# Cross-attention in a fused two-layer kernel: the sixth projection of a unit directly behind the fifth, both groups of outer key products behind it

## The reference

```python
q_hk  = (hidden_q @ Wq.T).reshape(Bv, Sv, H, K)          # H = 16 heads, K = 128
q_big = jnp.einsum('bshk,hkq->bshq', q_hk, w_kc_q)        # q = 192
q_big = _apply_rope(q_big, sin_q, cos_q)                  # rotary embedding
kv_r  = _apply_rope(kv_c, sin_k, cos_k)
q_r = jnp.einsum('bshq,hqr->bhsr', q_big, W_qr)           # r = 64
k_r = jnp.einsum('bld,hdr->bhlr', kv_r, W_kr)
attn = softmax(jnp.einsum('bhsr,bhlr->bhsl', q_r, k_r))
ctx_c = jnp.einsum('bhsl,bld->bhsd', attn, kv_r)
# then w_kc_kv, the heads side by side, and @ Wo.T
```

## Time and profile before

| | |
|---|---|
| median of 3 runs | 454.44 us (454.17 to 456.39) |
| profiled execution | 456.93 us, of which 455.1 us are the span |
| PE busy | 371.9 us, 82% of the span |
| DVE busy | 337.4 us, 74% |
| ACT busy | 212.2 us, 47% |
| POOL busy | 138.8 us, 31% |
| loop over the 8 units | about 212 to 363 us of the span |
| mean granted PE clock | 0.929 |

### The profile page before, as it was taken

How to read it: one execution, slowest core, us unless ns; L and a number is a source line. 1 busy time by engine, 2 the same in 40 slices (tenths; PEclk the granted TensorE clock), 3 DMA queues, 4 the chain that set the end, 5 groups by cost and what they waited for, 6 DMA issues and landing times.

```text
span 455.1 us, 10577 instructions
## 1 busy us (share of the span) xinstructions
PE 371.9 (82%) x3676; PEld 255.3 (56%) x3677; DVE 337.4 (74%) x858; ACT 212.2 (47%) x466; POOL 138.8 (31%) x149
## 2 busy tenths in 40 slices
PE   2578667832777788998999999999999989729995
PEld 1356555731344445776466475575664778616784
DVE  6968899888788989589677886886876525682453
ACT  1788999551577788684021231132132221324441
POOL 1100000023477774311092340440431410143334
PEclk9988999955599999998999999999999989957999
DMA  8995760402146551271022032032021101333011
GB/s 284 414 378 202 269 266 5 164 24 63 36 146 211 200 162 48 61 263 39 0 94 94 2 94 94 1 94 75 20 94 34 61 1 48 140 85 101 25 36 37
DMA packets 17183, 50.77 MB, mean 112 GB/s; under 512 B 2104, under 2 KB 6464, under 8 KB 15088
## 3 DMA queue, kind: packets, MB, share of 16 engines
q1 hardware_dynamic: 14272, 42.46, 25.9%
q0 software_dynamic: 2864, 7.68, 5.7%
HBM read 43.44 MB, written 6.69 MB: 110 GB/s over the span
## 4 chain that ended last, share of the span: by engine, by line
PE 58%; DVE 18%; ACT 9%; issue 7%; POOL 5%; DMA 2%; DVEq 0%; SPq 0%; ACTq 0%; POOLq 0%
PE bank L960 16%; PE bank L1174 8%; PE bank L976 6%; PE bank L1048 5%; PE bank L987 3%; ACT W L1207 2%; ACT pnat L1193 2%; PE bank L666 2%; PE bank L819 2%; PE bank L1001 2%; POOL y_rows L592 2%; PE bank L1027 2%; PE bank L1011 2%; PE bank L699 2%; PE bank L830 1%
## 5 line engine op out<-in xcount | busy, mean ns | idle before, releaser
L1722 DVE TENSOR_TENSOR roped<-bank,cst 128x512 f32<-128x512 f32 x96 | 61.1, 685 | 28.9 <-PE bank L960 27.9
L613 POOL TENSOR_TENSOR WE<-WE,wT 128x512 f32<-128x512 f32 x32 | 42.1, 1342 | 82.2 <-DMA WE<-_L_ffn_expert_masks_dram 82.2
L960 PE MATMUL bank<-XNT_hi,AW_hi 128*128 128x512 f32 x96 | 42.1, 438 | 0.0
L960 PE MATMUL bank<-XNT_lo,AW_hi 128*128 128x512 f32 x96 | 37.8, 394 | 0.0
L960 PE MATMUL bank<-XNT_hi,AW_lo 128*128 128x512 f32 x96 | 37.6, 392 | 0.0
L1341 ACT ACTIVATE qrT<-bank 128x512 f32<-128x512 f32 x16 | 8.7, 595 | 61.8 <-PE bank L987 61.8
L1048 PE MATMUL bank<-VW,ctxT 128*128 128x256 f32 x128 | 32.2, 399 | 0.0
L976 PE MATMUL bank<-roped,MW 128*64 128x512 f32 x128 | 31.0, 605 | 0.0
L1335 ACT ACTIVATE prob<-prob 128x512 f32<-128x512 f32 x16 | 10.1, 632 | 44.3 <-DVE prob L1732 44.3
L585 POOL DMA_INDIRECT xg<-x_rows,owner_b x23 | 22.7, 985 | 23.0 <-DVE owner_b L429 13.9
L960 PEld LDWEIGHTS bank<-XNT_hi,AW_hi 128*128 128x128 f32 x96 | 18.1, 188 | 19.4 <-issue 11.4
(11 more groups left out here) (306 smaller groups left out, 876.9 us busy)
## 6 DMA issues: line engine op xcount, KB each, us to landing
raw<-in_L_ffn_w_dram SPq DMA_DIRECT2D x8, 1536.0 KB, 8.4
fold<-in_L_xattn_fold_dram SPq DMA_DIRECT2D x8, 1024.0 KB, 5.6
WE<-_L_ffn_expert_masks_dram SPq DMA_DIRECT2D x8, 1024.0 KB, 5.4
kv<-in_keys_values_dram SPq DMA_DIRECT2D x8, 656.0 KB, 7.8
yg<-y_rows SPq DMA_DIRECT2D x8, 256.0 KB, 4.8
x_tok<-pay SPq DMA_DIRECT2D x8, 256.0 KB, 2.2
X<-in_x_dram SPq DMA_DIRECT2D x4, 256.0 KB, 9.9
x_rows<-xrow SPq DMA_DIRECT2D x1, 516.0 KB, 4.4
```

Source lines behind the costliest of these rows:

```text
L613: pool.tensor_tensor(WE[:, e], WE[:, e], wT[:], ALU.mult).then_inc(WE_ready, 1)
L960: mm = pe.matmul(bank[g][:], a[:, k, c * P:(c + 1) * P], b[:, k, g * 512:(g + 1) * 512], start=k == 0 and i == 0, stop=k == 1 and i == 2)
L1722: ins = dve.tensor_tensor(roped[n][:, r, :].rearrange("p (b s) -> p b s", s=S), src, cst[:, None, at:at + S].to_broadcast([P, 8, S]), ALU. ...
```

## The change

In PE's loop over the units, `project(u, 5)` is moved in front of `to_keys_outer(u, 0)`. Nothing else is changed, and no other engine's list.

```diff
@@ -1082,8 +1082,8 @@
                 project(u, 2)
                 project(u, 3)
                 project(u, 4)
+                project(u, 5)
                 to_keys_outer(u, 0)
-                project(u, 5)
                 to_keys_outer(u, 1)
                 to_keys_middle(u)
                 if u + 1 < NU:
```

## The result

The changed kernel takes 459.6 us (median of 4 runs, 457.96 to 462.76) against 454.31 us (4 runs, 454.13 to 456.39) on the same chip: a ratio of 1.0117, 95% interval 1.0076 to 1.0157, 5.3 us slower. The forecast was 460.1.

The account below looks back on a forecast made before the run. PE alone was taken to set the time in units 1 to 6, with DVE's work hidden. Units 1 to 6 +5.67, unit 0 -0.15, unit 7 +0.11: +5.63 on 454.44 gives 460.1 us, range 458.2 to 462.9.

Parts of the forecast that it names:

- The place and the kind of the wait: Units 1 to 7: projection 5, now directly behind projection 4, waits for rope 3 on DVE to free bank 1.
- The size of the wait: Unit 3: projection 5 starts 0.06 behind rope 3's end, at 272.91 instead of 271.96; the unit becomes 0.95 us longer.
- the sign to look for: Units 1 to 7: projection 5's load shows about 1.0 us of idle in front, released by rope 3.
- That it comes back in every unit: Units 1 to 6: rope 3 keeps its distance to the unit's start, so the wait recurs: 6 x 0.945 = 5.67 us.
- The joint of the two outer groups: Units 1 to 7: outer groups 0 and 1 back to back, up to 0.10 cheaper or dearer than 1.86; taken as 0.
- Unit 0: No wait, since no less_max stands ahead of rope 3; shorter by 0.10 to 0.20 from fewer matmul switches, taken as -0.15.
- Unit 7: Last unit of the loop: turn_probs starts at 350.85 instead of 350.74, +0.11 in place of 0.94.
- The turn from "DVE is late" to "PE is late": Unit 7: turn_probs stood idle 0.75 for by_sum; after the change probabilities are ready at 349.8 and PE is late.
- The sum: Whole kernel: 5.67 - 0.15 + 0.11 = +5.63 us, forecasting 460.1 us, 1.2% slower.
- The clock rival: Pauses of 0.95 in seven units lower PE's clock, up to 1.65 us each: 471.6 us; chance 0.05.
- the expert stage's 1.26 of idle without a drop: Evidence against the clock rival: from 145 to 147 PE idles 1.26 us and the clock stays at 1.00.
- The gain rival: No wait if rope 3 ends by 271.80 in unit 3: 8 x 0.15 + 0.75 = 1.95 us faster, 452.5; chance 0.05.

Follow-up runs that it names:

- two ways: Changed kernel with rope 3 moved before the second less_max on DVE: 0.9906; changed kernel with projection 5 and rope 5 in bank 7: 0.9883.
- both controls: Kernel before with rope 3 moved before the second less_max on DVE: 1.0030; kernel before with projection 5 and rope 5 in bank 7: 1.0000.
- rope 3 first: Changed kernel with the next unit's rope 3 moved on DVE in front of the second less_max: 452.23 us, ratio 0.9906.
- a free bank: Changed kernel with projection 5 and rope 5 in PSUM bank 7 instead of bank 1: 451.39 us, ratio 0.9883.
- the changed kernel with the 1.17 us operation: Changed kernel plus an unused 512-column multiplication by 1 on DVE before rope 3 of units 1 to 7: 469.60 us, ratio 1.0279.
- the one with 1.05: Changed kernel plus an unused 256-column multiplication by 1 on DVE before rope 3 of units 1 to 7: 469.96 us, ratio 1.0291.
- The three changed kernels with an added operation: Changed kernel plus an unused DVE operation before rope 3: 512-column multiplication by 1, 1.0279; 256-column, 1.0291; product of two SBUF operands, 1.0321.
- the kernel before with the 1.05 us operation: Kernel before plus an unused 256-column multiplication by 1 on DVE before rope 3 of units 1 to 7: 456.33 us, ratio 1.0034.
- The 512 columns: Unused 512-column multiplication by 1 on DVE before rope 3 of units 1 to 7: kernel before with it 1.0011, changed kernel with it 1.0279.
- the product: Unused product of two SBUF operands on DVE before rope 3 of units 1 to 7: kernel before with it 1.0052, changed kernel with it 1.0321.

## Why the prediction was right, point by point

**The place and the kind of the wait: right.** Projection 5 of units 1 to 7 waits for bank 1, released by rope 3. Shown by taking the wait away in two ways, and by both controls.

**The size of the wait: right.** I had rope 3's end + 0.06; it was 0.05. Projection 5 starts 5.56 behind projection 2 (275.76 - 270.20), where I had 272.91 - 267.33 = 5.58. Only the sign to look for was misstated: "about 1.0 us of idle" in front of projection 5's load is 1.29, and 0.86 in front of its matmul.

**That it comes back in every unit: right.** Rope 3 keeps its distance to projection 2, 4.23 before (271.56 - 267.33) and 4.22 after (274.42 - 270.20). The idle time that DVE has won went in front of the next unit's rope 0: 2.66 us in unit 3 (284.52), where the kernel before has 0.93 (280.84); 0.92 of it comes from rope 5, which waits 0.56 instead of 1.48.

**The joint of the two outer groups: mis-sized.** I took 1.86 + 1.87 = 3.73 and allowed 0.10 to either side; they take 3.58 together. With it the middle products start 10.73 behind projection 2 instead of 10.89. A unit costs 0.82 instead of 0.945, and the sum for units 1 to 6 is 4.9 instead of 5.67. The rows allow an estimate of the joint: eight outer matmuls more take 3.58 - 1.86 = 1.72, 0.215 each, so the step out of a group takes 1.86 - 7 x 0.215 = 0.36. Two groups in a row have one such step less, 0.36 - 0.215 = 0.14. The 1.86 that I took for a block held this step; the joint wasn't looked at by itself.

**Unit 0: -0.32 where I took -0.15.** The same 0.15 of the joint is what is missing.

**Unit 7: -0.03 where I took +0.11,** again short by the joint. The turn from "DVE is late" to "PE is late" came as worked out: the probabilities are ready 0.95 before turn_probs.

**The sum:** +4.54 in the loop by the trace against +5.63, and 5.3 (3.5 to 7.1 by the interval) by the runs. The better agreement with 5.6 of the second is luck, since runs of one kernel spread by 2 to 6 us.

**The clock rival: wrong for this change.** PEclk is 1.00 in all seven pauses of 0.86. Which side the trace of before pointed to (the expert stage's 1.26 of idle without a drop) was the right one. The experiments show that the rival is real at longer pauses, and that its price was near, 1.5 to 1.6 us a drop where it had up to 1.65. Even in the longer ones it takes a share of the pauses, not all. The Trainium skill's rule on pauses between groups of matmuls ("TensorE: Matmul & The Clock Gate", section "A second HAM failure mode: psum-queue depth-cycling") is not borne out by 0.86 us of pause, and is by about 2 us, in 7 of 17 pauses.

**The gain rival: wrong for this change; its condition was right, its price too low.** It asked for rope 3 to be over before 271.80, with about 2 us of gain in return. With rope 3 first the condition holds, with a free bank it isn't needed, and the kernels are 4.3 and 5.3 us faster by the runs, 3.4 and 3.5 by the loop in the trace. The loop shows 0.32 per unit where the rival had 0.15, for the joint once more, and 1.15 in unit 7 (12.64 to 11.49) where it had 0.15 + 0.75.

## What to carry to other kernels

Before two producers of the same double buffer are put back to back, look at how long the consumer still holds the first one's half: here the 1.86 us of work between them was the cover for a rotation that ended 0.9 before it was due. A new order is worth what its new neighbours wait for, so pair it with the edit that frees the buffer (an idle bank here), and test that edit alone as well. Fewer switches between kinds of matmul were a gain of 0.3 us per unit here, once nothing waited.

## What the runs showed of the hardware that I had not expected

**The granted clock falls after some pauses of about 2 us, not after shorter ones.** The two rows are windows of the changed kernel with the 1.17 us operation, behind the pauses of units 4 and 6; the third is of the one with 1.05, behind unit 2's pause of 1.95.

```profile
296.00:299.00 3.00, 3.00 (x8) 1.58 (x8) 1.29 (x4) 0.00 (x0) 0.00 (x0) 0.50 0.00 0
337.00:340.00 3.00, 3.00 (x8) 1.63 (x8) 1.25 (x4) 0.00 (x0) 0.00 (x0) 0.50 0.00 0
```

```profile
258.00:261.00 3.00, 3.00 (x8) 1.20 (x8) 1.55 (x4) 0.00 (x0) 0.00 (x0) 0.52 0.00 0
```

The three changed kernels with an added operation show 21 pauses. Around 7 of the 17 that lasted 1.87 to 2.37 us PEclk went from 1.00 to 0.50, from 2.4 to 1.2 GHz; around the four of 1.18 to 1.62 it did not, nor around the changed kernel's seven of 0.86. A drop cost 1.5 to 1.6 us: the period was 21.27 instead of 19.70. Among the longer ones length didn't decide: in units 2 to 6 it fell 3 times in 5 at 1.95, 2 at 2.08 and 2 at 2.35. What decided which of them is open.

**A multiplication that works in SBUF alone waits on DVE for POOL's running operation.** All three added operations took about 0.77 us more in units 2 to 6 than in unit 1: 0.42 and 1.18, 0.28 and 1.05, 0.68 and 1.45. The rows are the kernel before with the 1.05 us operation, in unit 2, the same operation in unit 1, and again in unit 7:

```profile
251.55 2.52 POOL L613 TENSOR_TENSOR WE<-WE,wT 128x512 f32<-128x512 f32 x2
...
253.17 1.05 DVE L1789 TENSOR_SCALAR w_raw<-w_raw 128x256 f32<-128x256 f32 x1
```

```profile
235.48 0.28 DVE L1789 TENSOR_SCALAR w_raw<-w_raw 128x256 f32<-128x256 f32 x1
235.52 5.12 POOL L613 TENSOR_TENSOR WE<-WE,wT 128x512 f32<-128x512 f32 x4
```

```profile
341.71 1.30 POOL L613 TENSOR_TENSOR WE<-WE,wT 128x512 f32<-128x512 f32 x1
...
342.50 0.66 DVE L1789 TENSOR_SCALAR w_raw<-w_raw 128x256 f32<-128x256 f32 x1
```

In unit 2 POOL's operation is done at 254.07, and the DVE operation ends 0.15 later; in unit 1 it had started before POOL began on its masks. In unit 7 it starts later within POOL's operation, waits only 0.38, and again ends 0.15 behind it (343.01 and 343.16). The 512 columns end 0.28 to 0.29 behind POOL's operation and the product 0.55, each the later by its own longer time. So the wait isn't a fixed amount, but what is left of the operation that POOL has begun. The trace of the kernel before shows the same behind the loop, where by_sum meets POOL's masks:

```profile
358.72 0.68 DVE L1736 TENSOR_REDUCE s_stat<-prob 128x8 f32<-128x512 f32 x1
359.21 1.26 POOL L613 TENSOR_TENSOR WE<-WE,wT 128x512 f32<-128x512 f32 x1
359.43 0.20 DVE L1737 RECIPROCAL s_stat<-s_stat 128x8 f32<-128x8 f32 x1
359.67 1.35 DVE L1738 TENSOR_TENSOR prob<-prob,s_stat 128x512 f32<-128x512 f32 x1
```

The product takes 1.35 instead of 0.69 and ends 0.55 behind POOL's operation (361.02 and 360.47), while the sum and the reciprocal, which also work in SBUF alone, keep their 0.68 and 0.20. The ropes, which read PSUM and one SBUF operand, take 1.29 with POOL at work and without. The Trainium skill agrees for the products: its page "GPSIMD Engine Reference", section "1. Specifications", has POOL sharing its SBUF interfaces with VectorE, in contention with operations of two SBUF inputs or in a two-port mode. Whether the multiplication by a constant, with its one SBUF input, ran in such a mode is shown by no run here.
